# Graph scores added up in memory by accumulating transfers, with the edge count as a fifth value

## What is computed

```python
xl = (x @ W_l).reshape(N, HEADS, HEAD_DIM)      # N = 625, HEADS = 4, HEAD_DIM = 64
xr = (x @ W_r).reshape(N, HEADS, HEAD_DIM)
e = xl[src] + xr[dst]
e = jnp.where(e >= 0, e, NEG_SLOPE * e)
score = jnp.einsum('ehd,hd->eh', e, att)        # 4 scores for each edge
m = jax.ops.segment_max(score, dst, num_segments=N)
ex = jnp.exp(score - m[dst])
alpha = ex / (segment_sum(ex, dst)[dst] + SM_EPS)
agg = segment_sum(alpha[:, :, None] * xl[src], dst)
```

## Time and profile before

| | |
|---|---|
| median of 3 runs | 1161.55 us |
| span of the profiled execution | 1154.3 us, its mean granted clock 0.912 |
| nearest of the three runs | 1156.02 us |
| blank tables ready, first turn of POOL | 68.63 us |
| first late turn | 232.57 us |
| last scatter issued | 515.86 us |
| attention of layer 0 done, experts begin | 604 us |

### The profile page before, as it was taken

How to read it: one execution, slowest core, us unless ns; L and a number is a source line. 1 busy time by engine, 2 the same in 40 slices (tenths; PEclk the granted TensorE clock), 3 DMA queues, 4 the chain that set the end, 5 groups by cost and what they waited for, 6 DMA issues and landing times.

```text
span 1154.3 us, 19240 instructions
## 1 busy us (share of the span) xinstructions
PE 948.9 (82%) x6532; PEld 829.5 (72%) x6532; DVE 858.0 (74%) x1953; ACT 466.5 (40%) x795; POOL 463.7 (40%) x374
## 2 busy tenths in 40 slices
PE   4586998879989998983835999985898588599996
PEld 2566886768978887853734999974588377589885
DVE  5659468869777978997987888776688765866635
ACT  1453755467858686616621111110253053212120
POOL 2448888877777877860001222250000000211104
PEclk9888999789999999997865999997999698699999
DMA  8962222323222232209704999983000000588883
GB/s 295 276 194 64 56 69 68 74 48 73 63 62 62 63 77 47 48 11 247 189 1 137 324 316 333 316 299 116 0 1 1 1 1 1 211 307 304 297 317 91
DMA packets 57946, 157.58 MB, mean 137 GB/s; under 512 B 23797, under 2 KB 32938, under 8 KB 49618
## 3 DMA queue, kind: packets, MB, share of 16 engines
q1 hardware_dynamic: 26830, 125.59, 33.3%
q0 software_dynamic: 25056, 24.10, 9.3%
q10 hardware_dynamic: 5992, 7.04, 1.7%
HBM read 136.50 MB, written 19.86 MB: 135 GB/s over the span
## 4 chain that ended last, share of the span: by engine, by line
PE 33%; DMA 24%; DVE 17%; POOL 12%; issue 10%; SPq 3%; POOLq 0%; ACT 0%; DVEq 0%; ACTq 0%
DMA pair_scores<-sc_ring,idx_ring 13%; PE bank L775 11%; PE bank L786 6%; POOL pair_scores L2153 5%; POOL arena L2143 5%; DMA arena<-pair_scores 4%; PE bank L544 3%; PE bank L708 2%; POOL arena L2208 2%; PE bank L496 2%; SPq L2232 2%; DMA arena<-slot_y,sloti 2%; DMA arena<-in_exp 1%; PE bank L697 1%; PE bank L874 1%
## 5 line engine op out<-in xcount | busy, mean ns | idle before, releaser
L2198 POOL DMA_INDIRECT arena<-row_tab,ids x42 | 57.7, 1373 | 493.7 <-DVE ids L1563 486.6
L2153 POOL DMA_INDIRECT pair_scores<-sc_ring,idx_ring x160 | 210.2, 1314 | 60.3 <-issue 43.4
L2143 POOL DMA_INDIRECT arena<-xl_tab,idx_ring x120 | 157.6, 1313 | 81.3 <-issue 31.7
L775 PE MATMUL bank<-arena 128*128 128x128 f32 x1480 | 180.8, 280 | 3.2 <-DMA arena<-in_exp 3.0
L775 PEld LDWEIGHTS bank<-arena 128*128 128x128 f32 x1480 | 175.0, 197 | 5.3 <-DMA arena<-in_exp 4.1
L1888 ACT ACTIVATE arena<-fmaps,node_neg 125x875 f32<-125x875 int32 x100 | 100.1, 1022 | 34.5 <-PE bank L544 34.5
L786 PE MATMUL bank<-arena 128*128 128x256 f32 (+1 forms) x404 | 97.6, 384 | 1.2 <-DMA arena<-in_exp0o 1.2
L1892 ACT ACTIVATE late_ohT<-arena 125x875 fp32r<-125x875 f32 x100 | 90.6, 926 | 0.0
L2021 ACT ACTIVATE arena<-bank 128x512 f32<-128x512 f32 (+2 forms) x76 | 34.4, 453 | 126.6 <-PE bank L775 126.5
L544 PE MATMUL bank<-late_hi,late_ohT 125*125 125x256 f32 x500 | 83.7, 298 | 0.6 <-DVE arena L1035 0.6
L786 PEld LDWEIGHTS bank<-arena 128*128 128x128 f32 (+1 forms) x404 | 72.1, 190 | 14.9 <-issue 6.0
(11 more groups left out here) (357 smaller groups left out, 2017.4 us busy)
## 6 DMA issues: line engine op xcount, KB each, us to landing
arena<-in_exp SPq DMA_DIRECT2D x25, 1024.0 KB, 7.1
arena<-in_exp SPq DMA_DIRECT2D x17, 1386.0 KB, 6.1
arena<-in_exp0o SPq DMA_DIRECT2D x25, 512.0 KB, 7.3
pair_scores<-cnt SPq DMA_DIRECT2D x10, 1093.8 KB
arena<-in_exp1o SPq DMA_DIRECT2D x17, 640.0 KB
fmaps<-in_rows SPq DMA_DIRECT2D x20, 437.5 KB, 3.8
arena<-pair_scores SPq DMA_DIRECT2D x7, 1093.8 KB
slot_y<-arena ACTq DMA_DIRECT2D x34, 128.0 KB, 6.4
```

The lines of the kernel that those rows point to most:

```text
L775: mm = pe.matmul(banks[1 + 2 * q + buf][0:rows, i * SLOTS:(i + 1) * SLOTS], w_in(s, q, k, m, rows), xsT[:, s, k, :], start=(k == 0), stop= ...
L2143: p.indirect_dma_start(out=gat[:, b % 2, 0, j * D:(j + 1) * D], out_offset=None, in_=xl_tab, in_offset=bass.IndirectOffsetOnAxis(ap=idx_ri ...
L2153: p.indirect_dma_start(out=pair_scores[which], in_=sc_ring[:, b % 2, j, :], in_offset=None, out_offset=bass.IndirectOffsetOnAxis(ap=idx_ri ...
L2198: p.indirect_dma_start(out=xs[:, q, :], out_offset=None, in_=tab, in_offset=bass.IndirectOffsetOnAxis(ap=ids[:, q, :], axis=0))\
```

## The change

Scores are now added into their cells, with an edge count as a fifth value, and the tables start as 0 with a count of 1e-15. Since one transfer cannot add twice to a cell, DVE finds the "twins" in each column of 125 edges: the last edge of a cell carries score times number of twins, and the number, and the others go to spare cells behind the table. For this each group's cell numbers are read as rows on all partitions (`cell_row`, stored once, then a broadcast of 2.5 KB to each of 128 partitions for every group). The count one-hots, the count products and everything that read them are gone. Groups are late from 8 on (`LATE` = 8), with three made columns and two gathers. ACT makes 4 of the 5 one-hot tiles of a late group and DVE the fifth; ACT also takes a fifth of the made rows (`fifth`). The second table is added onto the first in SBUF by accumulating transfers that POOL issues, in halves; DVE divides by the count.

```diff
-LATE = 12
-BEHIND = 4
-PIECES = [(0, 1), (3, 4), (2,)]
-MADE = PIECES[1]
-FETCH_AFTER = (0, 2, 3)
+LATE = 8
+PIECES = [(0, 1), (2, 3), (4,)]
+MADE = PIECES[1] + PIECES[2]
+FETCHED = list(PIECES[0])
+FETCH_AFTER = (0, 2)
...
+            def count_twins(g, b, ch):
+                s = b % 2
+                dve.wait_ge(sem(f"cells{s}"), g * 8 + (16 - 8 * s))
+                for j in range(G):
+                    ch.note(v.scalar_tensor_tensor(twin_junk[j], cell_row[0:P, s, j * P:(j + 1) * P],
+                                                   cellf[:, bass.ds(g * G + j, 1)], twin_weight[:, :], ALU.is_equal,
+                                                   ALU.mult, accum_out=twins[:, j:j + 1]))
...
+            def write_cells(g, b):
+                v.tensor_tensor(idx_ring[:, b % 4, 1, :], cell_kept[:, :], cell_spare[:, :], ALU.add)
...
+            def head_sums(ch, s, b, rows):
+                ch.link(v.tensor_reduce(sums[:, :, 0:H], rows.rearrange("p (g h c) -> p g h c", g=G, h=H), AX.X, ALU.add))
+                v.tensor_tensor(sc_ring[:, s, :, :], sums[:, :, :],
+                                times[:, b % 4, :].unsqueeze(2).to_broadcast([P, G, HR]), ALU.mult)\
+                    .then_inc(sem("scored"), 1)
...
-                weigh(scored_rows).then_inc(sem("z_read"), 1)
+                weigh(scored_rows, att_early).then_inc(sem("z_read"), 1)
+                count_twins(g + 2, g + 2, early)
+                place_twins(g + 2, g + 2, early)
                 dve.wait_ge(sem("z_read"), (g + 1) * NP)
...
-                head_sums(s, scored_rows).then_inc(sem("scored"), 1)
+                head_sums(early, s, g, scored_rows)
+                write_cells(g + 2, g + 2)
                 copy_indices(g + 2, g + 2)
...
             def table_maxima(m):
-                dve.wait_ge(sem(f"sdense{m}"), 32 * len(PARTS))
-                first, second = (sdense[q] for q in SDENSE[m])
-                v.tensor_tensor(first, first, second, ALU.max).then_inc(sem("merged"), 1)
-                dve.wait_ge(sem("merged"), m + 1)
+                dve.wait_ge(sem(f"merged{m}"), MERGED)
+                pairs = sdense[SDENSE[m]]
+                own.link(v.reciprocal(rcount, pairs[:, :, H]))
+                own.note(v.tensor_tensor(pairs[:, :, 0:H], pairs[:, :, 0:H],
+                                         rcount.unsqueeze(2).to_broadcast([P, N, H]), ALU.mult))
                 dve.wait_ge(sem("log_met"), m + 1)
+                own.note(v.tensor_scalar(no_edge, cnt[:, m, :], -1.0, -BIG, ALU.is_lt, ALU.mult))
+                own.fence()
+                own.link(v.tensor_tensor(cnt[:, m, :], cnt[:, m, :], no_edge, ALU.add))
...
-            for m in range(T):
-                own.note(v.tensor_scalar(nmask[:, m, :], cnt[:, m, :], -1.0, -BIG, ALU.is_lt, ALU.mult))
-            own.fence()
-            for m in range(T):
-                own.note(v.scalar_tensor_tensor(cnt[:, m, :], cnt[:, m, :], HD ** 0.5, nmask[:, m, :], ALU.mult,
-                                                ALU.add))
...
                 p.indirect_dma_start(
                     out=pair_scores[which], in_=sc_ring[:, b % 2, j, :], in_offset=None,
-                    out_offset=bass.IndirectOffsetOnAxis(ap=idx_ring[:, b % 4, 2, j:j + 1], axis=0))\
+                    out_offset=bass.IndirectOffsetOnAxis(ap=idx_ring[:, b % 4, 1, j:j + 1], axis=0),
+                    compute_op=ALU.add)\
                     .then_inc(sem(f"scattered{which}"), 16)
...
+            for m in range(T):
+                pool.wait_ge(sem(f"sdense{m}"), 16 * len(PARTS))
+                for rows in PARTS:
+                    slot = sdense[SDENSE[m]][rows, :, :].rearrange("p n h -> p (n h)")
+                    for lo, hi in HALF:
+                        p.dma_start(slot[:, lo:hi], cells[1][m][rows, lo:hi], accum_op=ALU.add)\
+                            .then_inc(sem(f"merged{m}"), 16)
...
+            read_out(sp, "cellT")
+            sp.dma_start(cell_rows[0:128, :], fd[:, 0, 0:P]).then_inc(sem("cells_stored"), 16)
+            sp.dma_start(cell_rows[128:EC, :], fd[0:EC - 128, 1, 0:P]).then_inc(sem("cells_stored"), 16)
...
+            sp.wait_ge(sem("cells_stored"), 32)
+            load_cells(0, 0)
+            load_cells(1, 1)
...
             edge_rows(2, 0, 0)
             blank_table(1)
+            load_cells(2, 0)
+            load_cells(3, 1)
```

More of the change, by code:

```diff
@@ L401, in got, with row_bank @@
             return banks[b], free[b]
+        def row_bank(late, s, r):
+            return banks[r if late and s == 1 else T + r]
         def kept_sum(t):
@@ new lines, in late_group, with made_row @@
+                more = lambda n: not (isinstance(g, int) and g + n >= NG)
+                def made_row(r):
+                    dve.wait_ge(sem("fifth"), g * 2 + (r - 2 * LATE))
+                    return v.tensor_tensor(part_of(scored_rows, r), part_of(fetched, r), row_sums(r, 1, s), ALU.max)
+                n = 16 * len(FETCHED)
+                dve.wait_ge(sem(f"gathered{s}"), g * (n // 2) + (8 * LATE * G + n - n // 2 * (LATE + s)))
+                dve.wait_ge(sem("z_made"), g * NP + 1)
@@ new lines, in late_group @@
+                piece = part_of(fetched, 0)
+                v.tensor_tensor(piece, piece, row_sums(0, 1, s), ALU.add).then_inc(sem("z_read"), 1)
+                if more(1):
+                    hot_tile(g + 1, b + 1)
+                dve.wait_ge(sem("z_read"), g * NP + 1)
+                ch.note(leaky(fetched, FETCHED))
+                if more(2):
+                    count_twins(g + 2, b + 2, ch)
+                made_row(1).then_inc(sem("z_read"), 1)
+                ch.note(made_row(2))
@@ L1198, in _ @@
                     .then_inc(freed, 1)
+            dve.wait_ge(sem("cells_made"), 1)
+            dve.wait_ge(sem("iotas"), 9)
+            for g in range(2):
+                count_twins(g, g, early)
+                place_twins(g, g, early)
+                write_cells(g, g)
             score_early(0)
@@ L1880, in biased, with apart_tile, hot_tile @@
                             .then_inc(freed, 1)
-            def hot_rows(g, s, late):
+            def apart_tile(g, s, late, t):
+                a.activation(apart[late, s][:, t, :], edge_row[late, s][0:P, :], ACT.Abs,
+                             bias=node_neg[:, t:t + 1]).then_inc(sem("apart"), 1)
+            def hot_tile(g, s, late, t):
+                made = (T - 1) if late else T
+                act.wait_ge(sem("apart"), g * made + (LATE * (T - made) + t + 1))
+                return a.activation(hot[late, s][:, t, :], apart[late, s][:, t, :], ACT.Relu, scale=-1.0, bias=1.0)
@@ L1884, in hot_rows, with rows_ready @@
+            def rows_ready(g, s):
                 act.wait_ge(sem(f"rows{s}"), g * 8 + (16 - 8 * s))
                 after(act, sem("z_made"), g * NP - NP)
[L1886 to L1889 removed]
+            def hot_rows(g, s, late):
+                rows_ready(g, s)
+                tiles = (T - 1) if late else T
+                for t in range(tiles + 1):
+                    if t < tiles:
+                        apart_tile(g, s, late, t)
@@ L2026, in step @@
                         store(b - 1, 1 - s)
+                    if static and b == 2 and name == "e0":
+                        a.activation(cnt[:, :, :], cnt[:, :, :], ACT.Copy, scale=HD ** 0.5).then_inc(sem("log_met"), 1)
                     if static and b == 3:
@@ L2231, in blank_table, with load_cells @@
                     for rows in PARTS:
-                        sp.dma_start(cells[which][m][rows], cnt[rows, :, :].rearrange("p m n -> p (m n)")[:, 0:H * NC])\
+                        sp.dma_start(cells[which][m][rows], cnt[rows, :, :].rearrange("p m n -> p (m n)"))\
                             .then_inc(sem(f"blank{which}"), 16)
+                sp.dma_start(pair_scores[which][N * NC:, :], cnt[0:P, 0, 0:HR]).then_inc(sem(f"blank{which}"), 16)
+            def load_cells(g, s):
+                after(sp, sem("twins_met"), g - 1)
+                sp.sem_inc(sem("turn"), 1)
+                sp.dma_start(cell_row[:, s, :], cell_rows.rearrange("(g j) p -> g (j p)", j=G)[bass.ds(g, 1), :]
+                             .rearrange("a n -> (a n)").partition_broadcast(128)).then_inc(sem(f"cells{s}"), 16)
             def edge_rows(g, s, late):
                 after(sp, sem("rows_hot"), g - 1)
+                if late and not (isinstance(g, int) and g < LATE + 2):
+                    sp.sem_inc(sem("turn"), 1)
+                    sp.wait_ge(sem("tile_hot"), g - (LATE + 1))
+                    sp.sem_inc(sem("turn"), 1)
                 n = ROWS if late else G * P
@@ L2275, in _ @@
                 for s in range(2):
+                    load_cells(i * 2 + s, s)
                     edge_rows(i * 2 + s, s, 1)
```

445 lines of the change are left out of this document (164 added, 281 removed).

## The result

| | before | changed |
|---|---|---|
| median of 4 runs each | 1163.01 us (1156.02 to 1166.98) | 1274.16 us (1272.65 to 1277.3) |
| span of the profiled execution | 1154.3 us | 1271.9 us |
| mean granted clock | 0.912 | 0.843 |

The ratio is 1.0962, with a 95% interval of 1.0918 to 1.1005: the changed kernel is 9.6% slower. I had forecast 1180 us and a range up to 1232; the direction was right, the size far too small, and the time lies outside the range.

A forecast was written before the change was run, and what follows sets the result against it. POOL was taken to pace early and late turns, with PE nearly full in the late ones. Edges -15 us, layer 0's attention +33 and layer 1 0 gave +18 us of span, 1180 us on the median; range 1143 to 1232.

The forecast's parts named there:

- The start: Before POOL's first turn: more loading, a lull and DVE's wait for the cell row start it 22 us later, near 90.6.
- Early turns: POOL's six early turns: 16.4 us each, with turn 3 waiting 4 us more, ending at 193 us.
- POOL: 7 transfers instead of 8, 7 x 1.50: POOL's work in a late turn: 10.5 us, plus 0.35 of stretch and a 1.1 us stall, 12.0 us in all.
- the landing: Time until an adding scatter has landed: 4.1 us taken, bounds 2.54 and 6.7, stalling each late turn by 1.1 us.
- a rival, at 0.4 us and 0.13: Scatters: descriptors take 0.4 us longer or landing takes 6 us; late turns 14.0 to 15.1, time 1225 to 1250 us; chance 0.13.
- faster* rival: Scatters: the added row lands within 3.0 us, no gap stalls, late turns 10.9 us, time 1145 to 1150 us; chance 0.2.
- The attention: Attention of layer 0: later first merged tile +10, DVE's work +28, less 4.5 of vanishing waits, together +33 us.
- DVE's part: Attention of layer 0: reciprocal of 4.0 us, product, mask and sum add 5.6 us on each of five tiles, +28 us.
- The term for the first merged tile: Attention of layer 0: first merged tile 23.5 us after the last scatter, before 13.5, so +10 us.
- The half-rate rival: Attention of layer 0: accumulation runs at half rate, DVE starves in tile 1, +57 us, time 1204 us; chance 0.2.
- Layer 1 and the rest: Behind layer 0's attention: the mask's ten operations leave DVE but lay under PE's products, so 0 us.

## Why the prediction was wrong, by its steps

**The start: right.** 90.64 us against 90.6, with DVE waiting 21.1 us for `cell_row` in front of it. That it agrees to 0.1 us is luck, since the start differs by some 6 us between runs. That 4 of the 22 us are DVE's work behind the last transfer was shown by the runs that moved it.

**Early turns: 20.0 us instead of 17.1 with the stall, +18 us.** 10 of these are the adding (120.2 against 110.3 us for six turns with plain scatters). The other 8, from 102.4 to 110.3, are DVE's twins, which I had costed for the late turns and not for the early ones, done behind cell rows that come late. The split depends on the order: with early cell rows the adding is worth 16.5 of them (118.9 us against 102.4), since POOL's own 19.2 us a turn then cover the rest.

**The step that failed: "POOL: 7 transfers instead of 8, 7 x 1.50".** I took a scatter's 1.20 us on POOL for the adding one too, and put all that was unknown about it into the landing. That was bounded, 2.54 to 6.7 us with 4.1 chosen, and 3.8 came out; but it had no effect. The issue had no bounds at all in the sum. It appeared as a rival, at 0.4 us and 0.13, with the row against it that gather and scatter take the same 1.2 us. That compares sizes of rows, and the cost goes by the number of rows and doubles with the adding, so it was no evidence. It is now 2.0 us: a late turn is 2 x 1.54 + 5 x 2.30 = 14.6 us instead of 12.0, 24 turns cost 66 us more, and the tail 2. With plain scatters the late turns take 12.17 us, near my 12.0, but that is luck. I let a landing of up to 3.0 us pass without a stall; a plain scatter lands after 3.0 us in the median, by which the sum gives 10.9, and the 0.9 us from the landing to the next scatter's start stood in no term. So the *faster* rival, 3.0 us and no stall, had a wrong condition too.

The Trainium skill bears on this, on the very page that I cited for the rate. "Collectives: The Full Stack", section "The bandwidth ceiling", says that a reducing transfer gets as many read descriptors as it has source addresses, two where a copy has one. The 9.1 ns a row against 4.7 fit that, but no run here shows the descriptors themselves. That POOL writes more of them for an adding scatter is my reading of the 1.98 us, not a measurement.

**The attention: +48 instead of +33.** DVE's part was right: 4.07 us for the reciprocal, 15.0 us from tile to tile with no gap. The term for the first merged tile was wrong, 39 us instead of 23.5. I gave the accumulating part half of the engines; it got 24%, beside the loads of the other tiles that had been issued at once. The half-rate rival would have given +57 with gaps on DVE; there were none, so it was neither.

**Layer 1 and the rest: right,** 532.0 against 533.5 us. The lower mean granted clock, 0.843 against 0.912, cost nothing that can be told behind the attention.

**The range.** The case that came true was among the rivals, at up to 1250 us. A price of 0.4 us stood for an operation that no row showed, on the engine that paced everything. The upper bound should have been the doubled transfer.

## What to carry to other kernels

A transfer of a kind that no row shows can cost the engine that issues it more, and not only land later. Where that engine is the pacer, bound the issue on both sides first, and the landing after it, with the time from a landing to the next start. Here 0.8 us on each of 160 scatters undid the removal of 800 products on PE and of one POOL transfer in eight. The one transfer that everyone waits for got a quarter of the bytes beside loads that had been issued at once. Holding all of them back was no cure, 11 us slower; fetching plainly and adding on DVE was as good as accumulating. And moving work into a cheaper phase can take away the cover of what lay beside it, as in the run with late groups from 8 on.

## What the hardware showed

- An adding scatter of 125 rows took POOL 1.98 us, a plain one 1.20; 64 rows took 1.43 and 0.92. Four or five values of 4 bytes made no difference.
- It landed 3.8 us after its start (median), a plain one 3.0. A plain scatter that had to wait for the landing of the one before started 0.90 us after that landing (0.79 with 64 rows).
- Accumulating 1.56 MB from memory into SBUF took 12.4 us alone, 9.0 us plainly, and 27.5 us beside the loads of other tiles.
- `RECIPROCAL` took 4.07 us for 625 elements, 6.5 ns each; ACT's exponential of the same took 0.73 us.
- The page counts 121174 packets for the changed kernel and 59734 with plain scatters, 384 more for each adding scatter. With 64 rows it was 48 more, and plain scatters of 64 rows counted as many as those of 125, so I rest nothing on the count.
- Why, with plain scatters, the first scatter of a turn landed after some 4.4 us and others after 3.0 stays open.
